# A four-layer graph network: later edge chunks in packed windows with own slots, row sums on ScalarE

## The reference

```
edge_index = jnp.stack([src, dst])
x = _layernorm(x + _L0_gnn_ref(x, src, dst, edge_weight, L0_gnn_W), axis=-1)
x = _layernorm(x + _L1_gnn_ref(x, edge_index, L1_gnn_W1, ...), axis=-1)
x = _layernorm(x + _L2_gnn_ref(x, src, dst, edge_weight, L2_gnn_eps, ...), axis=-1)
x = _layernorm(x + _L3_gnn_ref(x, edge_index, L3_gnn_W, ...), axis=-1)
# L0, L2: agg = segment_sum(edge_val[:, None] * x[edge_col], edge_row), then products
# L1: two convolutions (128 and 64 wide), each: h = x @ W; out = segment_sum(h[s] * norm, d); batch norm, relu
# L3: one convolution, 256 wide, layer norm, relu
```

## Time and profile before

| | |
|---|---|
| median of three runs | 3434.12 us (3432.56 to 3437.37) |
| the profiled execution, its time | 3437.37 us |
| its span | 3436.1 us |
| busy: PE, DVE, ACT, POOL | 2833.6, 2051.0, 1009.4, 2503.3 us |
| mean granted TensorE clock | 0.913 |
| HBM | 434.19 MB read, 214.52 MB written |

### The profile page before, as it was taken

The page is one execution under the profiler, slowest core; times in us unless marked ns, Lnnn a source line. Parts: engine busy times, 40 slices in busy tenths (PEclk is TensorE's granted clock), DMA queues, the critical chain, the costliest instruction groups (busy, mean ns, idle before and its releaser), DMA issues. The chain is left out here.

```text
span 3436.1 us, 59943 instructions
## 1 busy us (share of the span) xinstructions
PE 2833.6 (82%) x19203; PEld 2096.4 (61%) x19220; DVE 2051.0 (60%) x7385; ACT 1009.4 (29%) x2549; POOL 2503.3 (73%) x2237
## 2 busy tenths in 40 slices
PE   5989888888888869789968887678788875699995
PEld 4767666566777648444447774366676664466664
DVE  7899988887888638342253334433444564245557
ACT  4343444445666438100010003400111232001123
POOL 3888888887777666677747777777777774777773
PEclk9999999999999979899969996589999988799997
DMA  8777888888999889788847876755565554988884
GB/s 274 113 140 102 157 158 155 152 152 182 187 186 181 176 221 313 193 217 236 236 105 201 225 219 176 228 155 156 167 181 174 166 170 137 291 234 248 250 251 137
DMA packets 658433, 652.77 MB, mean 190 GB/s; under 512 B 87902, under 2 KB 606476, under 8 KB 656588
## 3 DMA queue, kind: packets, MB, share of 16 engines
q0 software_dynamic: 153600, 258.41, 37.7%
q1 hardware_dynamic: 430670, 331.83, 31.3%
q10 hardware_dynamic: 73854, 58.70, 5.4%
HBM read 434.19 MB, written 214.52 MB: 189 GB/s over the span
## 5 line engine op out<-in xcount | busy, mean ns | idle before, releaser
L1691 POOL DMA_INDIRECT A<-rows_buf,big x572 | 940.2, 1644 | 272.4 <-issue 155.3
L885 POOL DMA_INDIRECT rows_buf<-T,idx x888 | 851.7, 959 | 276.0 <-issue 273.9
L979 PE MATMUL PSA<-S,rows_buf 128*128 128x128 bf16 (+2 forms) x5904 | 585.8, 254 | 221.9 <-DMA rows_buf<-X,idx 103.8
L979 PEld LDWEIGHTS PSA<-S,rows_buf 128*128 128x128 bf16 (+2 forms) x5904 | 525.4, 143 | 303.8 <-DMA rows_buf<-X,idx 93.3
L1035 DVE TENSOR_TENSOR accT<-PSA,accT 128x256 f32 (+2 forms) x354 | 132.7, 375 | 837.8 <-PE PSA L979 830.8
L885 POOL DMA_INDIRECT rows_buf<-X,idx x528 | 508.9, 964 | 161.0 <-issue 157.6
L1381 PE MATMUL PSA<-XRS,rows_buf 128*128 128x256 f32 x1144 | 312.6, 397 | 3.9 <-DMA XRS<-in_xpad 3.9
L1547 DVE TENSOR_TENSOR accT<-PSA,accT 128x392 f32 (+5 forms) x366 | 239.2, 654 | 76.7 <-PE PSA L1478 41.4
L1393 ACT ACTIVATE rows_buf<-PSA 128x512 f32<-128x512 f32 x286 | 169.2, 594 | 225.9 <-PE PSA L1381 212.4
L1381 PEld LDWEIGHTS PSA<-XRS,rows_buf 128*128 128x128 f32 x1144 | 210.7, 197 | 30.4 <-issue 5.2
L796 ACT ACTIVATE accT<-accT,vec 128x500 f32<-128x500 f32 (+3 forms) x26 | 17.7, 693 | 668.4 <-DVE accT L794 668.3
(11 more groups left out here) (316 smaller groups left out, 5540.6 us busy)
## 6 DMA issues: line engine op xcount, KB each, us to landing
XRS<-Ad SPq DMA_DIRECT2D x400, 256.0 KB
Ad<-accT SPq DMA_DIRECT2D x224, 196.0 KB
XRS<-in_xpad SPq DMA_DIRECT2D x192, 128.0 KB, 4.1
Awd<-accT SPq DMA_DIRECT2D x48, 392.0 KB
A<-accT SPq DMA_DIRECT2D x9, 1600.0 KB
rows_buf<-T,idx POOLq DMA_INDIRECT x888
rows_buf<-A SPq DMA_DIRECT2D x24, 512.0 KB
accT<-A SPq DMA_DIRECT2D x24, 512.0 KB, 6.3
```

Source lines behind the costliest of these rows:

```text
L885: s_hg[slot(i)][j // 2].on(pool.indirect_dma_start(Gv(slot(i), j), None, table, bass.IndirectOffsetOnAxis(idx[:, c:c + 1], 0)), 16)
L979: last = pe.matmul(PS[bank_of(i)][0:F, W * h:W * h + W], Gv(slot(i), j)[:, o:o + F], hits[:, i % SRING, j, :], start=j + part == 0, stop=j ...
L1691: s_k[n].on(pool.indirect_dma_start(A, bass.IndirectOffsetOnAxis(tgt[:, c:c + 1], 0), G[:, i % RING, j, :], None, compute_op=ALU.add), 16)
```

## The change

Chunks from 404 (window 16) on lie in *packed* windows: eight windows of nine chunks with 14 slots each and eight of eight chunks with 16 slots each, so that 28 windows become 32 and end at chunk 540 instead of 524. In a packed window each chunk has its own slots, whether or not targets of neighbours coincide. So a unit's result is copied into the buffer and not added: the first 25 blocks by VectorE, the other 24 by ScalarE straight out of PSUM, and nothing is cleared. In return the quad's result has to be added chunk by chunk (`packed_quad`). Apart from that, the row sums of the equal sources are made by ScalarE in all steps, from one compare of 512 columns on VectorE, and `targets` moves to the start of the next step. `cnt` is zeroed once and `ones` shrinks.

```diff
-NWIN = 28
+NATURALS = 16
+PACKS = ((8, 9, 14), (8, 8, 16))
+NWIN = NATURALS + sum(m for m, _, _ in PACKS)
@@ place_units
-    cost = lambda u: 1.15 + 0.67 * u.k if u.hot else 0.2 + 0.051 * u.n + u.k * (0.35 + 0.0128 * u.n)
+    cost = lambda u: 1.15 + 0.67 * u.k if u.hot else 1.35 if u.packed else 0.2 + 0.051 * u.n + u.k * (0.35 + 0.0128 * u.n)
@@
+    pool.memset(cnt[:, :, :], 0.0)
@@ hybrid
+        def packed_quad(q):
+
+            if by_rows is None:
+                s_hdn.by(v, D0 + PQ * (q + 1))
+            else:
+                s_tp.by(v, T0 + q + 1)
+            bank = 2 + 2 * (q % pairs) if by_rows is None else 6
+            units = [(j, c) for j in range(per) for c in range(BND[per * q + j], BND[per * q + j + 1])]
+            for k, (j, c) in enumerate(units):
+                if k % LOADREGS == 0:
+                    lo = c - PACKED
+                    los = nc.values_load_multi_w_load_instructions(
+                        ubi[0:1, lo:min(lo + LOADREGS, BND[per * q + per] - PACKED)], engines=[ET.DVE], min_val=0, max_val=LAST,
+                        skip_runtime_bounds_check_because="held under LAST")[1]
+                slots = WIDTHS[per * q + j - NATURALS]
+                aw = acc(los[k % LOADREGS])[:, 0:slots]
+                at = 512 * bank + W * j + slots * (c - BND[per * q + j])
+                s_hacc.by(v)
+                s_hqa.by(v)
+                s_hqa.on(v.scalar_tensor_tensor(aw, PSA[0:F, at:at + slots], okf[0:F, 0:1], aw, ALU.mult, ALU.add))
+
         def quad(q):
+            if per * q >= NATURALS:
+                packed_quad(q)
+                return
@@ window_out
+                if w >= NATURALS:
+                    s_ca.of(sp, ("unit", FINAL[w].at))
@@ equals
-            for j in range(CG):
-                last = v.tensor_scalar(Eq[:, i % 2, j, :], PS[0][:, 128 * j:128 * j + 128], srcf[:, g, j:j + 1], 0.0,
-                                       ALU.is_equal, ALU.add, accum_out=cnt[:, g, j:j + 1])
-            last.then_inc(s_eq, 1)
+            v.tensor_tensor(Eq[:, i % 2, :, :], PS[0].rearrange("p (j e) -> p j e", j=CG),
+                            srcf[:, g, :].unsqueeze(2).broadcast_to([128, CG, 128]), ALU.is_equal).then_inc(s_eq, 1)
+
+        def row_sums(i):
+
+            sc.wait_ge(s_eq, i + 1)
+            for j in range(CG):
+                last = sc.activation(junk[:, j, :], Eq[:, i % 2, j, :], ACT.Identity, accum_out=cnt[:, G0 + i, j:j + 1])
+            last.then_inc(s_rs, 1)
@@ targets
-            v.wait_ge(s_eq, i + 1)
+            v.wait_ge(s_rs, i + 1)
@@ unit_copy
-            if u.halved:
+            if u.packed:
+                sc.wait_ge(s_amw, NUW + u.half + 1)
+                if u.first:
+                    before = user_before(u.w)
+                    sc.wait_ge(s_aw[TURN[before] % 2], 16 * PARTS * (TURN[before] // 2 + 1))
+                got = PS[7][:, 0:(NT - FIRSTHALF) * u.n].rearrange("p (b s) -> p b s", s=u.n)
+                s_ca.mark(("unit", u.at), sc.activation(pack_slots(u)[:, FIRSTHALF:NT, :], got, ACT.Identity))
+            elif u.halved:
@@ unit_out
+            if u.packed:
+                v.wait_ge(s_ae, u.turns[0])
+                if u.first:
+                    before = user_before(u.w)
+                    v.wait_ge(s_aw[TURN[before] % 2], 16 * PARTS * (TURN[before] // 2 + 1))
+                v.wait_ge(s_am, u.at + 1)
+                got = AB[:, 0:FIRSTHALF * u.n].rearrange("p (b s) -> p b s", s=u.n)
+                v.tensor_copy(pack_slots(u)[:, 0:FIRSTHALF, :], got).then_inc(s_ae, 1)
+                return
@@ the loop over steps, ScalarE, at the end of step i
+            if i + 1 < NCOLD:
+                row_sums(i + 1)
@@ the loop over steps, VectorE
             additions(us[0:1])
+            targets(i)
             if i + 1 < NCOLD:
                 equals(i + 1)
...
-            if i + 1 < NCOLD:
-                targets(i + 1)
```

More of the change, by code:

```diff
@@ L53, in window_bounds @@
     b, last = [0], 0.0
-    for w in range(1, NWIN + 1):
+    for w in range(1, NATURALS + 1):
         c = E / 128 * math.sqrt((last + SPAN) / N)
@@ L58, in window_bounds @@
         last = N * (b[-1] * 128 / E) ** 2
+    for m, k, _ in PACKS:
+        for _ in range(m):
+            b.append(b[-1] + k)
     return b
@@ L64 @@
 HOT = BND[NWIN]
+PACKED = BND[NATURALS]
 FAR = 16384
 CLASSES = ((0, 64, 4, 8), (64, 120, 2, 8), (120, 160, 2, 10), (160, HOTW, 1, 8),
-           (HOTW, 376, 2, MAXN), (376, 448, 1, 14), (448, HOT, 1, 16))
+           (HOTW, 376, 2, MAXN), (376, PACKED, 1, 14))
+WIDTHS = [n for m, _, n in PACKS for _ in range(m)]
 G0 = BND[XWIN] // CG
@@ L81, in __init__ @@
         self.hot = w < HWIN
+        self.packed = w >= NATURALS
 def natural_units():
@@ L89, in natural_units @@
             us.append(Unit(c, k, next(w for w in range(NWIN) if c < BND[w + 1]), n))
+    for w in range(NATURALS, NWIN):
+        us += [Unit(c, 1, w, WIDTHS[w - NATURALS]) for c in range(BND[w], BND[w + 1])]
     for i, u in enumerate(us):
@@ L114 @@
 for i, u in enumerate(HALVED):
-    turns += [(u, 0)] + [(HALVED[i - 1], 1)] * (i > 0)
-turns.append((HALVED[-1], 1))
+    turns += [(u, 0)] + [(HALVED[i - 1], 1)] * (i > 0 and not HALVED[i - 1].packed)
 for u in UNITS:
@@ L126, in window_range, with sums_of @@
 def window_range(w):
-    at = N * (BND[w] * 128 / E) ** 2
-    return max(0, math.floor(at) - 125), min(LAST, math.ceil(at) + 125)
+    at, last = (N * (c * 128 / E) ** 2 for c in (BND[w], BND[w] if w < NATURALS else BND[w + 1] - 1))
+    return max(0, math.floor(at) - 125), min(LAST, math.ceil(last) + 125)
+def sums_of(q, per):
+    return sum(1 if w < NATURALS else BND[w + 1] - BND[w] for w in range(per * q))
 def unit_at(p):
@@ L179 @@
 DENSE0 = cleared_at(HWIN - 1, 3) + 1
-CLEARED = [w for w in ORDER if w >= HWIN and any(user_before(q) == w for q in range(NWIN))]
+CLEARED = [w for w in ORDER if w >= HWIN and any(user_before(q) == w for q in range(NATURALS))]
 FARBLOCK = window_range(HWIN)[0] // 128
@@ L495, in build @@
         least, most = window_range(w)
-        done = v.tensor_scalar(wb[:, lo:hi], cm[:, lo:lo + 1].broadcast_to([128, hi - lo]), float(least), float(most), ALU.max, ALU.min)
+        starts = cm[:, lo:lo + 1].broadcast_to([128, hi - lo]) if w < NATURALS else cm[:, lo:hi]
+        done = v.tensor_scalar(wb[:, lo:hi], starts, float(least), float(most), ALU.max, ALU.min)
     link(done)
     s_d.by(sc)
-    for w in range(NWIN):
-        first = sc.activation(bwi[0:1, w:w + 1], wb[0:1, BND[w]:BND[w] + 1], ACT.Identity)
-    s_q.on(first)
+    for w in range(NATURALS):
+        sc.activation(bwi[0:1, w:w + 1], wb[0:1, BND[w]:BND[w] + 1], ACT.Identity)
+    s_q.on(sc.activation(ubi[:, :], wb[0:1, PACKED:HOT], ACT.Identity))
     hot16 = cur16[:, 0:G0, :]
@@ L515, in scatter_rows @@
         link(v.tensor_scalar(spare[:, :, :], srcf[:, :, :], -1.0, pidx[:, 0:1], ALU.mult, ALU.add))
+    widths = [(lo, hi, n) for lo, hi, k, n in CLASSES]
+    widths += [(BND[w], BND[w + 1], WIDTHS[w - NATURALS]) for w in range(NATURALS, NWIN)]
     def unit_places_known():
@@ L907, in product @@
                 if by_rows is None:
-                    s_hqa.by(pe, Q0 + per * (q - pairs + 1))
+                    s_hqa.by(pe, Q0 + sums_of(q - pairs + 1, per))
                 else:
@@ L950, in turn @@
             if q:
-                s_hqa.by(pe, Q0 + per * q)
+                s_hqa.by(pe, Q0 + sums_of(q, per))
             for j in range(per):
@@ L1145, in slice_added @@
             if q >= 0:
-                s_hqa.by(v, Q0 + per * (q + 1))
+                s_hqa.by(v, Q0 + sums_of(q + 1, per))
         def added(engine, t):
             if last_quad(block[t]) >= 0:
-                s_hqa.by(engine, Q0 + per * (last_quad(block[t]) + 1))
+                s_hqa.by(engine, Q0 + sums_of(last_quad(block[t]) + 1, per))
             if last_group(block[t]) >= 0:
@@ L1719, in additions @@
                 unit_out(u)
-                if u.halved and u.half:
+                if u.halved and u.half and not HALVED[u.half - 1].packed:
                     unit_out(HALVED[u.half - 1], 1)
-                if u is HALVED[-1]:
-                    unit_out(u, 1)
         equals(0)
@@ L1727, in spread @@
         scatter_rows()
-        targets(0)
         for i in range(NCOLD):
@@ L2031, in f @@
         def f():
-            remaining(BND[(NWIN, 16, HWIN)[i]] // CG)
+            remaining(BND[(NWIN, NATURALS, HWIN)[i]] // CG)
             link(v.tensor_reduce(left[:, i:i + 1], cur[:, :, :], AX.XY, ALU.max))
```

20 lines of the change are left out of this document (13 added, 7 removed).

## The result

| | before | changed |
|---|---|---|
| median | 3434.22 us (3432.56 to 3437.37, 4 runs) | 3561.03 us (3553.8 to 3566.83, 4 runs) |
| ratio | | 1.0358, 95% interval 1.034 to 1.0377 |
| profiled execution, its span | 3437.37, 3436.1 us | 3553.8, 3552.6 us |

The forecast was 3541 us, slower, in a range of 3465 to 3605. The trace divides the 116.5 us between the two spans as follows; a stage of aggregation is taken from its first to its last group addition (an addition into `accT` of one group's 128 columns, L1079 after).

The account below looks back on a forecast made before the run. Bounds: GpSimd's scatters, then SyncE's store queue; GpSimd's gathers in the aggregations, TensorE close behind. Terms 54 - 8 + 2 + 22 + 17 + 20 = +107 us on 3437.4 gave 3544, median 3541 us; range 3465 to 3605.

Parts of the forecast that it names:

- Window stores: Scatter stage: 15 window periods at 22.2 us in SyncE's store queue, 333 us against 279.3, +54 us.
- Engines' relief: Scatter stage: less VectorE work, with row sums on ScalarE, gives back GpSimd's waits, -8 us (ends 0 and -18).
- Bursts: Aggregations: a packed quad's 36 or 32 small VectorE additions take 21.6 or 19.2 us, low end 16.
- the register load: VectorE bursts: one load per four additions, taken at 0.965 us, making four additions cost 2.4 us.
- The stall terms: First aggregation: TensorE waits for one-hots behind three bursts, 6.5 + 10.4 + 5.4 = +22 us.
- upper bound of 35: First aggregation: stalls reach 35 us if TensorE's granted clock falls to 1.2 GHz after each.
- First aggregation: Eighth quad eats four groups' gain, TensorE becomes the bound, +2; stalls +22; bare last burst +17 us.
- Second aggregation: Four groups less -20 us; three bursts holding TensorE +23; bare last burst +17; together +20, from 2 to 35.
- Only the bursts: Rival: window parts land at 20 us a window or relief arrives early, bursts still cost; 3498 us, chance 0.13.
- only the queue: Rival: store queue costs, but bursts are 16 us with loads of 0.35 us; 3490 us, chance 0.10.
- Faster: Rival: SyncE stops bounding the scatter stage, windows every 15.4 us, bursts 16 us; 3388 us, chance 0.08.
- Worse: Rival: streams of windows slow the aggregations' gathers too; 3620 us, chance 0.03.

Follow-up runs that it names:

- kernel before with four parts: Kernel before with each window stored in four parts of 400 KB, not eight of 200 KB: 3430.47 us, ratio 0.9968.
- the run with wide additions: Changed kernel with each packed quad added by four 128-column additions, not 32 or 36 narrow ones (wrong sums, timing only): 3481.59 us, ratio 1.0117.
- the same two cures: Changed kernel with window stores in four parts and packed additions spread over five steps: 3818.67 us, ratio 1.0008, second chip.

## Why the forecast held, step by step

**Window stores, +54.** Right: the same mechanism, 22.4 us a window for 22.2, the same queue. Larger stores and fewer windows each take it away, 48 and 47.5 us. The Trainium skill (DMA: Bandwidth & Descriptors, "Anatomy of one DMA") states, for transfers that GpSimd issues, a fixed cost per transfer whatever its size. Here SyncE issues them: halving the number of parts at equal bytes took a window's period from 22.4 to 18.2 us, and a part of 392 KB lands 3.7 us after its issue (kernel before with four parts, 890 to 1200 us) where one of 196 KB takes 2.8 (changed kernel), so for this queue too the trace agrees in kind.

**Engines' relief, -8.** 8 to 17 us by window 16, so right or too small; the end of 18 that the earlier trace rows had set was not passed. The row sums alone are worth 10 us of the whole.

**Bursts, 21.6 and 19.2 us.** The spacing was right, the register load was the mis-sized term. I took 0.965 us, from the load at L1042, because the new loads stand right behind an addition; measured 0.343 us and 0.15 us of added spacing, as at the quad's old place. Standing right behind an addition didn't make the load dear. Bursts were 16.7 and 14.8 us, near the low end of 16. The stall terms by the same steps: 7.3 + 5.3 + 2.3 instead of 6.5 + 10.4 + 5.4, and the last 13.8 instead of 17. I had the clock's fall only as an upper bound of 35; it came, and cost some 3.5 us.

**First aggregation, +2 + 22 + 17 = +41.** Measured 43.8, but by luck in part, as two errors cancel: the bursts gave 32 (14.9 + 13.8 + 3.5; 33 by the run with wide additions) for 39 and the base +11 for +2. The base went wrong in the step from TensorE's need to the stage's pace. I set 290 us over 53 steps, 5.47 each, from matmuls back to back, and counted the rest as unchanged. Measured are 5.54 us a group from the first addition on (20 up to 1558 us) and 5.72 later.

**Second aggregation, -20 + 40 = +20.** Measured +36.3. That TensorE would "catch up slowly" at 4.8 us a step, behind a GpSimd at 5.0, is the step that failed: it took 5.31 with 95% busy, so the four groups' 20 us came back only as 11 (the run with wide additions). Of the 5.31, 0.28 are waits for streamed matrices (9.3 us in 33 steps), the rest TensorE's own 5.03. The bursts cost 47 there and not 40: waits of 26.0 for 23 and a bare last burst of 13.4 for 17 nearly cancel, and the 7 above are by estimate the low clock, which no term of this stage held.

**Rivals.** Only the bursts (3498) and only the queue (3490) are both excluded, as each loss exists and has its own run. Faster (3388) would have needed a window every 15.4 us; even with four parts it took 18.2. Worse (3620), by streams slowing the gathers, is not seen on the first chip.

The changed kernel is slow for two reasons, shown by taking each away on the first chip: the queue 48 us and the bursts 79, against 10 us won by the row sums. What the eighth quad and four groups fewer leave in the aggregations is 10 us more in the first and 11 less in the second. Together that is some 116 us for the 116.5 between the spans, closer than these runs can tell; on the second chip the same two cures took away 76 us. The parts are not additive to the last us, as the row sums and larger stores together show.

## What to carry to other kernels

Before adding units of work that end in a transfer, count the transfers in the queue that issues them: a queue that waits for each landing has a fixed pace, and a plan that adds a seventh more items is late by that, whatever the engines save. When a wide operation is cut into many narrow ones, place them behind what another engine waits for, and see what the last batch lies bare to. A trade of gathered groups for streamed windows pays only as long as TensorE isn't the next bound; its need is to be read from a stretch where it is full, not from a sum of matmuls. And a stall of TensorE can cost more than its length: look at the granted clock of the work behind it.

## What was unexpected in the hardware

A register load on VectorE took 0.343 us (68 loads, 337 ns at least) right behind an addition, though the same kind of load at L1042 of the kernel before took 0.965 (and the same line, L1086, takes 0.965 in the changed kernel): the duration of a load isn't a property of its kind. Around stalls of 5.3 to 10.3 us TensorE's granted clock went to 0.50, and twelve matmuls that take 0.83 us elsewhere took 1.46; around one of 2.3 us it stayed at 1.00. The same kernel takes 3440 us on one chip and 3815 on another, nearly all of it, by the profiles above, in stages that stream and gather, and a change measures +3.6% on one and +2.2% on the other: ratios of a kernel that is bound elsewhere don't carry over.
